# Equal half blocks in a DLRM tower: pairs regrouped through DRAM, ten one-hot tables, a 128-column stationary

## What is computed

```python
e = jnp.stack([tbl_f[ids[:, f]] for f in range(27)], axis=1)
x = jnp.einsum('bfd,bgd->bfg', e, e).reshape(B, 27 * 27)[:, TRIL_IDX]   # 351 pairs
h = jnp.concatenate([bottom, x, bottom], axis=1)
h = jnp.maximum(h @ W_top1 + b_top1, 0.0)     # 607 x 512
h = jnp.maximum(h @ W_top2 + b_top2, 0.0)     # 512 x 256
y = h @ W_top3                                # 256 x 1
```

## Time and profile before

| what | value |
|---|---|
| median of 3 runs | 436.91 us (436.74 to 436.97) |
| the profiled execution | 435.65 us, span 433.8 us |
| PE (TensorE matmul) busy | 387.4 us, 89%, 2942 records |
| PEld (weight loads) busy | 358.8 us, 83% |
| DVE (VectorE) busy | 250.8 us, 58% |
| ACT (ScalarE) busy | 172.9 us, 40% |
| POOL (GpSimd) busy | 291.8 us, 67% |
| granted TensorE clock, mean | 0.961 |
| DMA | 35.87 MB, mean 83 GB/s |

### The profile page before, as it was taken

The page is one execution under the profiler, slowest core; times in us unless marked ns, Lnnn a source line. Parts: engine busy times, 40 slices in busy tenths (PEclk is TensorE's granted clock), DMA queues, the critical chain, the costliest instruction groups (busy, mean ns, idle before and its releaser), DMA issues.

```text
span 433.8 us, 8424 instructions
## 1 busy us (share of the span) xinstructions
PE 387.4 (89%) x2942; PEld 358.8 (83%) x2942; DVE 250.8 (58%) x764; ACT 172.9 (40%) x387; POOL 291.8 (67%) x311
## 2 busy tenths in 40 slices
PE   0756899999989599999999999999998895989997
PEld 0646798999979499897998999898998894968986
DVE  3756679653695258541687487453695593433251
ACT  2314273535423233443532534525433433232544
POOL 6777787777777777777777777777777777750000
PEclk9885999999999689999999999999999997999999
DMA  6999124323244233331334424223254222210000
GB/s 130 238 241 254 50 76 99 78 75 71 65 100 106 54 77 89 70 77 52 80 78 112 97 58 95 71 61 63 65 103 111 54 79 75 55 44 0 2 2 0
DMA packets 24340, 35.87 MB, mean 83 GB/s; under 512 B 8490, under 2 KB 17452, under 8 KB 24310
## 3 DMA queue, kind: packets, MB, share of 16 engines
q0 software_dynamic: 9728, 19.94, 17.7%
q1 hardware_dynamic: 12842, 13.77, 15.5%
q10 hardware_dynamic: 1740, 1.77, 1.6%
HBM read 35.45 MB, written 0.01 MB: 82 GB/s over the span
## 4 chain that ended last, share of the span: by engine, by line
PE 58%; POOL 16%; issue 7%; DMA 6%; DVE 6%; SPq 3%; ACT 2%; ACTq 2%; POOLq 0%; DVEq 0%
PE ps_gram L788 17%; POOL rows L414 16%; PE ps_build L759 15%; PE ps_dense L838 13%; PE ps_build L770 6%; DMA rows<-tbl_dram,idx 3%; DMA raw<-tbl_dram 3%; DVE hot L456 3%; PE ps_dense L814 2%; ACTq L559 2%; PE ps_dense L883 1%; PE ps_dense L831 1%; DVE gram L463 1%; SPq L312 1%; PE ps_gram L838 1%
## 5 line engine op out<-in xcount | busy, mean ns | idle before, releaser
L414 POOL DMA_INDIRECT rows<-tbl_dram,idx x304 | 291.0, 957 | 94.3 <-issue 89.0
L456 DVE TENSOR_SCALAR hot<-id_raw,vocab 125x256 fp32r<-125x256 int32 x512 | 160.1, 381 | 29.9 <-PE ps_build L759 18.8
L759 PE MATMUL ps_build<-hot,table 125*128 125x256 f32 x1024 | 144.1, 295 | 17.8 <-DVE table L431 11.4
L759 PEld LDWEIGHTS ps_build<-hot,table 125*128 125x128 f32 x1024 | 132.2, 198 | 23.4 <-issue 17.2
L788 PE MATMUL ps_gram<-embT 128*122 128x104 f32 x1024 | 120.6, 272 | 1.9 <-ACT embT L579 1.9
L788 PEld LDWEIGHTS ps_gram<-embT 128*122 128x122 f32 x1024 | 116.5, 190 | 6.2 <-issue 5.2
L463 DVE COPY gram<-ps_gram 32x208 f32<-32x208 f32 x128 | 46.7, 365 | 93.0 <-PE ps_gram L788 91.6
L770 PE MATMUL ps_build<-ident,rows 128*128 128x128 f32 x304 | 49.5, 287 | 22.2 <-DMA rows<-tbl_dram,idx 14.0
L594 ACT COPY gram<-ps_gram 32x208 f32<-32x208 f32 (+1 forms) x128 | 41.4, 323 | 56.6 <-PE ps_gram L788 55.8
L589 ACT COPY embT<-ps_build 128x512 f32<-128x512 f32 (+1 forms) x80 | 45.2, 566 | 44.5 <-PE ps_build L770 43.4
L770 PEld LDWEIGHTS ps_build<-ident,rows 128*128 128x128 f32 x304 | 37.0, 149 | 25.9 <-DMA rows<-tbl_dram,idx 13.1
(11 more groups left out here) (63 smaller groups left out, 147.1 us busy)
## 6 DMA issues: line engine op xcount, KB each, us to landing
id_raw<-ids_onehot_dram SPq DMA_DIRECT2D x32, 256.0 KB
rows<-tbl_dram,idx POOLq DMA_INDIRECT x304, 2.5
raw<-tbl_dram SPq DMA_DIRECT2D x8, 448.0 KB
bot<-bottom_dram SPq DMA_DIRECT2D x3, 256.0 KB, 2.6
w1p_raw<-w_pairs_dram ACTq DMA_DIRECT2D x1, 702.0 KB
w_raw<-w_dram ACTq DMA_DIRECT2D x1, 512.0 KB
raw<-tbl_dram SPq DMA_DIRECT2D x8, 52.0 KB
idx<-ids_dram SPq DMA_DIRECT2D x16, 13.5 KB, 1.8
```

Of the source, the lines that this page charges most:

```text
L414: nc.gpsimd.indirect_dma_start(rows[:, t % 2, s * D:(s + 1) * D], None, tables[f], bass.IndirectOffsetOnAxis(idx[:, t, f:f + 1], 0)).then_ ...
L456: last = nc.vector.tensor_scalar(hot[0:VP, q, v0, v, :], id_raw[0:VP, n % 2, q, :], vocab[0:VP, row:row + 1], None, ALU.is_equal)
L759: last = nc.tensor.matmul(bank[:, q * HALF:(q + 1) * HALF], table[0:VP, 2 * p + q, bits, row:row + D], hot[0:VP, q, v0, v, :], start=(v0 = ...
```

## The change

- The batch is worked on in eight equal halves of 256 samples. The dense part of half i - 1 runs inside half i, after the first tile's pair products. All dense products have 256 columns.
- Ten tables instead of eight are taken by one-hot products, so 17 are gathered. The order of a half is: one-hot pairs 0 and 1, then lookups of tile 0 between pairs 2, 3 and 4, two last banks of lookups, pair products of tile 0 with the lookups of tile 1, layer 1, and the pair products of tile 1 with layers 2 and 3 between them. One pair of one-hot rows is made ahead, during tile 1 of the half before.
- `relayout`, the packing and `pairs_back` are kept for the last half alone. For the others, SP writes `gram` (128 partitions) to a scratch in DRAM when both engines have filled it, and reads it back in 29 DMAs, one or two for each of 26 features, to `pairX` with pairs on partitions, in chunks of 120, 111 and 120 pairs. ScalarE waits for a chunk before it copies its high part, between the pair units of tile 0.
- The bottom rows come transposed from the host, so `bottom_back` goes. All later ids of gathered tables are loaded at once.
- The stationary of a pair product has all 128 columns, and `gram` 128 partitions.

```diff
-ONEHOT_TABLES = 8
-BLOCK, HALF, TILE = 512, 256, 128
+ONEHOT_TABLES = 10
+HALF, TILE = 256, 128
+HALVES = BATCH // HALF
...
+CHUNK_AT = (0, 120, 231, 351)
...
+    plan = ([("hot", 0), ("hot", 1), ("tile", 0, 0), ("hot", 2), ("tile", 0, 1), ("hot", 3), ("tile", 0, 2), ("hot", 4),
+             ("tile", 0, 3), ("tile", 0, 4)] + [("tile", 1, u) for u in range(TQ)])
...
-    GR = (GROUP - 1) * PAD + PG
+    GR = GROUP * PAD
...
+            def write_gram(i):
+                sp.wait_ge(gram_dve, GRAMS * (i + 1))
+                sp.wait_ge(gram_act, GRAMS * (i + 1))
+                sp.sem_inc(loads_begun, 1)
+                sp.dma_start(scratch[:, :], gram[:, :, :].rearrange("p n j -> p (n j)")).then_inc(gram_out, 16)
+            def read_pairs(i, some):
+                if 0 in some:
+                    sp.wait_ge(gram_out, 16 * (i + 1))
+                    sp.sem_inc(loads_begun, 1)
+                src = scratch.rearrange("(k r) (n j) -> r k n j", k=GROUP, n=PG)
+                for s in some:
+                    n, c, p, a, b = reads[s]
+                    sp.dma_start(pairX[p:p + b - a, c, :].rearrange("p (k j) -> p k j", k=GROUP),
+                                 src[a:b, :, n, :]).then_inc(pairs_in[c], 16)
+            def half(i, at, more=True):
+                next_ids(i, 0, at, 3)
+                write_gram(i - 1)
+                next_ids(i, 1, at, 4)
+                read_pairs(i - 1, range(len(reads)))
+                if more:
+                    next_ids(i, 2, at + HALF, 2)
+                next_bottom(i, at)
...
+            def half(i, more=True):
+                for p in range(1, OP):
+                    make_hot(i, p)
+                    if p == 1:
+                        bottom_low(i - 1)
+                for u in range(GU):
+                    empty_gram(i, 0, u)
+                    if u < 3:
+                        pairs_low(i - 1, u)
+                for m in range(M1):
+                    layer1_low(i - 1, m)
+                for u in range(GU):
+                    empty_gram(i, 1, u)
+                    if more:
+                        make_hot(i + 1, 0, [u])
...
+            def half(i):
+                features(i, i - 1)
+                first_tile(i, lambda u: pairs_high(i - 1, u) if u < 3 else None)
+                layer1(i - 1)
+                second_tile(i, lambda u: layer2(i - 1, u) if u < 2 else layer3(i - 1) if u == 2 else None)
...
-                                                embT[:, at:at + GROUP, :].rearrange("p k g -> p (k g)")[:, 0:GR],
+                                                embT[:, at:at + GROUP, :].rearrange("p k g -> p (k g)"),
...
+            def half(i):
+                features(i)
+                first_tile(i)
+                for m in range(M1):
+                    layer1_bottom(i - 1, m)
+                    layer1_pairs(i - 1, m)
+                pair_products(i, 1, 0, (0, 1))
+                layer2(i - 1, 0)
+                pair_products(i, 1, 1, (0, 1))
+                layer2(i - 1, 1)
+                pair_products(i, 1, 2, (0, 1))
+                layer3(i - 1)
+                pair_products(i, 1, 3, (0, 1))
...
-    nc = _bacc.Bacc("TRN2", target_bir_lowering=False, num_devices=1)
+    nc = _bacc.Bacc("TRN2", target_bir_lowering=False, num_devices=1, dynamic_dma_scratch_size=8192)
```

More of the change, by code:

```diff
@@ L153, in dlrm_tower, with use_1, use_2, use_y @@
     M1, M2 = H1 // 128, H2 // 128
[L155 to L166, removed]
+    reads = pair_reads()
+    CHUNK_READS = [len([r for r in reads if r[1] == c]) for c in range(3)]
+    DENSE = M1 + M2 + 1
+    TAIL = RG + 3
+    def use_1(i, m):
+        return (TAIL if is_half(i, LAST) else 0) + m
+    def use_2(i, m):
+        return use_1(i, M1 + m)
+    def use_y(i):
+        return use_1(i, M1 + M2)
     ctx = ExitStack()
@@ new lines, in _ @@
+            emb_tile(FIRST, 0, 3)
+            emb_tile(FIRST, 0, 4)
+            first_tile(FIRST, split_weights)
+            second_tile(FIRST, lambda u: split_weights(GU + u))
+            half(1)
+            with act.Fori(2, LAST) as i:
+                half(i)
+            half(LAST)
+            bottom_high(LAST)
+            for u in range(1, RG, 2):
+                act.wait_ge(densed, DENSE * LAST + u + 1)
+                for dst, src in pack_pieces(u):
+                    last = nc.scalar.copy(dst, src)
+                last.then_inc(pack_act, 1)
@@ L718, in _ @@
+            for c in range(3):
+                pairs_high(LAST, c)
             layer1(LAST)
@@ L885, in layer3, with relayout @@
                 last.then_inc(densed, 1)
-            def pairs_of_half(i, half, dense=None):
-                t = 2 * half
+            def relayout():
+                pe.wait_ge(gram_dve, GRAMS * HALVES)
+                pe.wait_ge(gram_act, GRAMS * HALVES)
+                for u in range(RG):
+                    bank = dense_bank(LAST, u)
+                    for n in range(u * RB, min((u + 1) * RB, PG)):
+                        last = nc.tensor.transpose(bank[0:J, (n % RB) * 128:(n % RB) * 128 + GR], gram[0:GR, n, :],
+                                                   ident[0:GR, 0:GR])
+                    last.then_inc(densed, 1)
@@ new lines, in pairs_back @@
+            def pairs_back():
+                pe.wait_ge(pack_dve, (RG + 1) // 2)
+                pe.wait_ge(pack_act, RG // 2)
+                for c in range(3):
+                    bank = dense_bank(LAST, RG + c)
+                    for k in range(GROUP):
+                        last = nc.tensor.transpose(bank[0:CHUNKS[c], k * J:(k + 1) * J],
+                                                   packed[0:J, k, CHUNK_AT[c]:CHUNK_AT[c + 1]], ident[0:J, 0:J])
+                    last.then_inc(densed, 1)
@@ new lines, in _ @@
+            pe.wait_ge(consts_made, 3)
+            features(FIRST)
+            pe.wait_ge(pad_set, 1)
+            first_tile(FIRST)
+            for u in range(GU):
+                pair_products(FIRST, 1, u, (0, 1))
+            half(1)
+            with pe.Fori(2, LAST) as i:
+                half(i)
+            half(LAST)
+            relayout()
+            pairs_back()
+            for m in range(M1):
+                layer1_bottom(LAST, m)
+            for m in range(M1):
+                layer1_pairs(LAST, m)
```

801 lines of the change are left out of this document (301 added, 500 removed).

## The result

The changed kernel takes 455.24 us (median of 4 runs, 454.0 to 456.56) beside 436.94 us for the kernel before (4 runs, 436.74 to 437.57): ratio 1.042, 95% interval 1.0395 to 1.045. It is slower, which was the likelier side, but by 18 us and not 7, and outside the range. In a later set of runs it took 456.08 beside 435.27: 1.048, 1.043 to 1.052.

What follows compares the result with a forecast made beforehand. GpSimd's gathers set the pace, TensorE close behind; then TensorE's halves: 69.8 to half 1, seven halves of 50.8 less 2.0, tail 18.0 less 0.3: span 441.1, median 444 us. Range 417 to 452, forecast's own 433 to 453.

Steps and rivals of the forecast that it cites:

- The bound moves from GpSimd to TensorE: Steady part: 272 gathers need 42.5 us a half, TensorE's half is longer, so GpSimd waits for TensorE.
- the 49 to 52: Length in us of a half, forecast 50.8; under 49 or over 52 would show the prediction wrong.
- The stationary, the slow class (0.1118): Pair products: 128-column load stays slow, pace rises from 0.1066 to 0.1118 us, 0.65 us a half more.
- Rival 1: Pair products: the 128-column load becomes fast, pace near 0.09 us, median 422 us; chance 0.36.
- The scratch hidden: Scratch write there at 9.3 us, last read at about 24.3, needed from 26.5 to 30.5: 6 us of cover.
- rival 3: Scratch reads come late, at 0.8 us each, every half waits 4.6 us more, 476 us; chance 0.07.
- Features, 24.3 us: One-hot and lookup stretch of a half, set by VectorE: 20.3 + 5.0 - 1.0; last half 2.0 less.
- the lower bound: Features of a half: TensorE's own 21.1 us plus two ScalarE copy waits of 0.43, making 22.0.
- the 1.0 of relief: Features: 1.0 us taken off because VectorE's operations come faster where GpSimd is idle, some 5 us.
- Rival 2: Features: VectorE keeps up, 22.0 us a half, median 430 us; chance 0.04.
- The head, 53.2: Start of the kernel: first pair products at 53.2 us instead of 51.16, bounds 51.2 and 58.6.
- the two upper bounds: Highest values allowed: head 58.6 us, with the added pair at full price; features 25.3 us a half, without relief.

Runs made afterwards that it cites:

- eight-table form: Changed kernel with pairs alternating over two banks, 122 columns, 128 rows written, weights' loads spread or on SP, eight one-hot tables for ten: 431.38 and 429.45 us.
- ten-table twin: Changed kernel with pairs alternating over two banks, 122 columns, all 128 rows written, weights' loads spread or on SP: 438.42 and 442.08 us.
- runs with full rows: Changed kernel with the pair products' stationary at 122 columns, all 128 rows still written to the scratch: 451.23 us.
- repaired form: Changed kernel with one-hot pairs alternating over two banks and lookups placed mid-pair: 444.49 us beside 456.08 unchanged.
- form with the weights out of the way: Changed kernel with weights' loads issued by SP behind all other loads, weight splits one eviction later: 457.85 us.

## Why the prediction was right and wrong

- **The bound moves from GpSimd to TensorE: right.** 272 gathers, GpSimd waiting for TensorE. The eight-table form shows the other side of that balance, 7 to 13 us faster than its ten-table twin. A half took 51.5 us, inside the 49 to 52 outside of which the prediction called itself wrong; the time left the range all the same.
- **The stationary, the slow class (0.1118): right.** Measured 192 ns and 0.111. Rival 1, the fast load, and with it 0.36 of chance and the range's whole lower part, is refuted: no pair product's load took less than 186 ns. The Trainium skill (TensorE: Matmul & The Clock Gate, section on LDWEIGHTS) prices a load at columns / 1.2 ns; by estimate that is 5.0 ns for the six columns. The runs with full rows give 4.8. For the whole load of 128 columns the same formula gives 107 ns, and the trace has 192.
- **The scratch hidden: right**, write, landing and reads within 1 us of the forecast, and rival 3 (late reads, 476 us) did not come. The sum had priced the write without asking how its rows fall on the engines. It was right at 128 rows; at 122 the same sum would have been wrong by 12 us a write and some 60 us in all, and not for the reads but for the load queued behind.
- **Features, 24.3 us: the step that failed.** Measured 25.4 on average, and 25.3 in the last half, for which the sum took 2.0 off. I counted VectorE's fifth pair and, for the lower bound, two copy waits of 0.43, but not on which bank each pair lies. The changed plan's waits (0.69, 0.26, 0.68, 0.33, 0.46) are there in every half and don't shrink when GpSimd falls silent. The form with banks in turn takes 0.65 a half less where no gather hangs. What is left, 24.4 to 25.2, is the limit I had argued for, so the 1.0 of relief was too much as well; the last half then takes 23.8, not 22.3. Where a gather hangs it is 22.1, my lower bound of 22.0. Rival 2 (VectorE keeps up, 22.0) came true in those halves of the repaired form alone. In the sum, 7 x 1.13 and the 2.0 are 9.9 us too little, less 3.0 by which the rest of the seven halves was shorter than forecast (26.05 against 26.5 each): the 6.9.
- **The head, 53.2: the other step that failed.** Measured 58.27, inside its bounds (58.6). The sum let TensorE's two added pairs start at 34.5 as before, and priced nothing for the loads of two more tables beside the same weights; TensorE went on at 38.28. The form with the weights out of the way gives 52.4, but the weights are then what is late. Which load holds the head stays open.
- **The range** ended at 452 (453 for the forecast alone), though the two upper bounds together give 444 + 5.4 + 7 x 1.0 = 456. The head came within 0.3 us of its bound and the features went 0.1 above theirs, with no relief in the last half: 5.1 and 9.9, less the 3.0 of the rest and with 0.4 elsewhere, are the 12.4 us of span.

## What to carry to other kernels

When a plan of uses over a few buffers changes, write down the buffer of each use again: "s mod 2" over a list that alternates two kinds gives every one of a kind the same buffer, and the wait is for its copy. Look at how many DMA engines a transfer keeps busy when it stands ahead of others in a queue (here 128 rows against 122), and ask of a slow one who is queued behind it, not only who reads it. A stretch in which two limits lie within a microsecond gives little when one is removed: 0.65 us a half here, and 3.4 to 3.5 where the second limit happened to be gone too.

## What was not expected of the hardware

- A write of 122 rows of 6.5 KB used 2 DMA engines and took 19 us to where its reads could start; 128 rows took 6.9.
- The issue behind the load of the gathers' row numbers (202.5 KB) took 8.1 us; with that load moved, 0.54 at the old place and 8.79 at the new one.
- A gather that starts after a wait for TensorE, while VectorE runs one-hot operations without a break, can take 6.8 to 12.9 us instead of 0.94, in each of the ten-table forms. In 48 of 65 cases it ends within 0.83 us after VectorE's operations break off. 48 of VectorE's operations took 14.97 us beside gathers and 12.71 without. Why the gather hangs stays open.
- In two sets of runs every form took 1.5 times as long, with waits of 5 to 25 us that no instruction of the program ended; there the changed kernel's forms were 1 to 3% faster than the kernel before. The chip number of the second set stands beside a later, undisturbed set as well. The cause was not found.
